# A graph layer on one core: its first two column chunks opened together, unit by unit

## The chip, the cores and the metric

The kernel runs on one core of one Trainium2 chip. The metric is the device time of one execution in microseconds (us), median of several. Beside the median stands one profiled execution, whose trace is read below. Engines are called PE (TensorE), ACT (ScalarE), DVE (VectorE), Pool (GpSimd) and SP (SyncE, which here issues the loads).

## The reference

With N = 4096 and D = 128, and one dense adjacency matrix `adj` [N, N] for both branches:

```
h   = max(layernorm(x), 0)
out1 = conv(h,  adj, eps1, W1, b1)
out2 = conv(x2, adj, eps2, W2, b2)
y   = x + concat(out1, out2) @ Wm.T + bm

conv(v, a, eps, W, b):
    ax = a @ v
    t = ax + (1 + eps) * ax
    for i in 0..2:  t = relu(t @ W[i].T + b[i])
    return t
```

Everything is float32.

## The kernel before

**Numbers.** To keep float32 accuracy, each operand of a product is split in two: a rounded part `hi` (type fp32r) and the rest `lo` = raw - hi. A product is three matmuls: lo x hi, hi x hi, hi x lo. `product` (L436 on; its matmuls are L440, L441, L444) does this.

**Tiles.** The output is made transposed, in 8 chunks of 512 columns (`CW`). For each chunk the 4096 rows to be summed are taken in 8 units of 4 blocks of 128 (`U`, `JB`). One unit of `adj` is 128 x 2048, 1 MB; it goes through a ring of 4 slots (`adj_raw`, `adj_hi`, `adj_lo`). The array `adj_tiles` holds each unit as 128 rows of 8 KB. Per unit and branch PE does 4 blocks x 3 matmuls of 512 columns, so 24 per unit and 192 per chunk, into the PSUM banks `acc[0]` and `acc[1]`. Branch 1 (x2) comes first in each unit, then branch 0 (x); after branch 0, `unit_used` frees the slot.

**Who does what for a unit.** SP loads it. ACT rounds it to `adj_hi` (L230 whole, L263 by block). DVE subtracts to `adj_lo` (L338 whole, L394 by block). PE multiplies.

**Features.** `feat_hi` and `feat_lo` hold all 32 blocks of both branches and are made once, during chunk 0, one unit of 4 blocks at a time. x2: ACT rounds (L268), Pool subtracts (L203). x: DVE takes `bn_stats`, `bn_aggr`, adds epsilon (L362, L365, L367); ACT the square root (L273); DVE a reciprocal with one Newton step (L373 to L378); ACT applies scale, shift and relu (L280, `rectify`) and rounds (L283); Pool subtracts (L207).

**Order of the work.** Each engine has its own instruction stream, written by hand, and the streams meet at semaphores. Chunk 0 is unrolled. In it SP issues, for each unit, x, x2 and then the unit of adj; the first three units (`FINE_LOADS`) are loaded as four DMAs of 256 KB, each 2 KB out of every 8 KB row. ACT does for each unit: x2's rounding, the square root, four adj_hi of 512 columns, `rectify`. DVE does: `variances`, `scale_and_shift`, four adj_lo of 512. PE's `first_aggregate` (L464, L470, L480) takes first all hi x hi of a unit and branch, then feat_lo x hi, then hi x adj_lo. Before the first product PE does 12 matmuls on zeros (`WARM_UP`, L550).

**Layers.** When a chunk's sums are ready, ACT drains them from PSUM twice, as `act_hi` and `act_f` (L246, L247, `branch_operand`), DVE makes `act_lo` (L344), and PE does a layer of both branches (6 matmuls, `layer`) after units 1, 3 and 5 of the next chunk and the merge after unit 6. `acc` is one pair of banks, so the first product of a chunk waits for `act_f` of the chunk before. The last chunk has an order of its own, with the second branch's layers in quarters of 128 columns. The weights are split by Pool after chunk 0's features (L210, L212).

Of the kernel before, what the change touches and what calls it, by code (L numbers as in the profile page):

```python
# [6 lines left out]
def gnn_layer_kernel(nc, adj_tiles, x_tiles, x2_tiles, x_t, w_t, bias_t, eps, out_t):  # L7
# [4 lines left out]
    ALU = mybir.AluOpType  # L12
# [5 lines left out]
    CW = 512  # L18
# [24 lines left out]
    OPERAND_AFTER = {1: 0, 3: 1, 5: 2, 7: 3}  # L43

# [11 lines left out]
    with ExitStack() as ctx:  # L56
# [46 lines left out]
        hidden_quarter = [hidden[0], bank("hidden_quarter1"), hidden[1], bank("hidden_quarter3")]  # L103
# [55 lines left out]
        def _(sp):  # L159
            def load_unit(c, u):  # L160

                if not (isinstance(c, int) and c * U + u < RING):
                    sp.wait_ge(lo_made, c * U + (u + 1 - RING))
                sp.dma_start(adj_raw[:, u % RING, :], adj_tiles[c * U + u]).then_inc(raw_loaded[u % RING], 16)
# [7 lines left out]
            for u in range(U):  # L172
                load_x(u)
# [3 lines left out]
                if u < FINE_LOADS:  # L177
                    for j in range(JB):
                        cols = slice(j * CW, (j + 1) * CW)
                        done = fine_loaded[u * FINE_SIGNALS + j] if j < FINE_SIGNALS else raw_loaded[u]  # L180
                        sp.dma_start(adj_raw[:, u, cols], adj_tiles[u][:, cols]).then_inc(done, 16)
                else:
                    load_unit(0, u)
                if u == U - 2:
# [3 lines left out]
            with sp.Fori(1, CHUNKS) as c:  # L188
# [8 lines left out]
        def _(pool):  # L197

            for u in range(U):
# [9 lines left out]
            pool.wait_ge(w_loaded, 16)  # L209
            nc.gpsimd.tensor_copy(w_hi[:, :, :], w_raw[:, :, :]).then_inc(w_hi_made, 1)  # L210
            pool.wait_ge(w_hi_made, 1)
            nc.gpsimd.tensor_tensor(w_lo[:, :, :], w_raw[:, :, :], f32(w_hi[:, :, :]),  # L212
                                    ALU.subtract).then_inc(w_lo_made, 1)
# [11 lines left out]
        def _(act):  # L225
            def high_of_unit(c, u):
                act.wait_ge(raw_loaded[u % RING], 16 * (c * (U // RING) + (u // RING + 1)))
                if not (isinstance(c, int) and c * U + u < RING):
                    act.wait_ge(unit_used, c * U + (u + 1 - RING))
                nc.scalar.activation(adj_hi[:, u % RING, :], adj_raw[:, u % RING, :], ACT.Copy).then_inc(hi_made, 1)  # L230

            def source(m, k, b):
# [21 lines left out]
            def fine_high(u, j):  # L254
                slot, cols = u % RING, slice(j * CW, (j + 1) * CW)
                last = j == FINE_SIGNALS
                if u < FINE_LOADS and not last:
                    act.wait_ge(fine_loaded[u * FINE_SIGNALS + j], 16)
                else:
                    act.wait_ge(raw_loaded[slot], 16 * (u // RING + 1))  # L260
                if u >= RING:
                    act.wait_ge(unit_used, u + 1 - RING)
                nc.scalar.activation(adj_hi[:, slot, cols], adj_raw[:, slot, cols], ACT.Copy).then_inc(  # L263
                    hi_made if last else fine_hi_made, 1)

# [24 lines left out]
            for u in range(U):  # L290
                high_of_x2(u)
                std_of_x(u)
                for j in range(JB):
                    fine_high(u, j)
                rectify(u)
            act.wait_ge(bias_loaded, 16)
            act.wait_ge(scale_made, 1)
            with act.Fori(1, LAST) as c:
# [25 lines left out]
        def _(dve):  # L324
# [294 lines left out]
```

## Time and profile before

| | |
|---|---|
| median of 3 runs | 414.39 us (414.32 to 414.98) |
| profiled execution | 414.23 us |
| its span, first to last instruction | 412.3 us |
| PE busy | 403.9 us, 98% |
| DVE busy | 221.1 us, 54% |
| ACT busy | 219.8 us, 53% |
| chain that ended last | PE 85%, DVE 6%, ACT 5%, issue 2%, DMA 1% |
| DMA | 76.15 MB, mean 185 GB/s |

The span is what the trace covers; the execution's time is 1.93 us longer. Matmuls are pipelined, and a record shows a matmul from its start to its modelled end, so the records overlap: the pace is the distance from start to start. Where a row of the timeline merges several instructions ("x4"), its time is from the first start to the last end.

### The profile page before, as it was taken

The page shows a single profiled execution, that of the slowest core. Times are in us where ns is not written, and L with a number is a line of the kernel's source. Part 1 is how long each engine was busy: PE and PEld are TensorE (multiplying, and loading weights), DVE is VectorE, ACT ScalarE, POOL GpSimd, SP SyncE. Part 2 cuts the span into 40 slices and gives each one's busy share as a digit, 9 for nine tenths or more (in the row PEclk, how much of TensorE's full clock was granted, in tenths as well). Part 3 has the DMA queues.
Part 4 walks back from the last instruction along what each step waited for, and adds up shares of the span by engine and source line. Part 5 has one row for each costly group of instructions (what it writes and reads, how often), then busy time and mean ns, then how long its engine had stood idle before and what let it go on. Part 6 is the DMA issues. An engine that isn't in the chain of part 4 may idle for free.

```text
span 412.3 us, 5004 instructions
## 1 busy us (share of the span) xinstructions
PE 403.9 (98%) x1763; PEld 326.9 (79%) x1763; DVE 221.1 (54%) x277; ACT 219.8 (53%) x276; POOL 34.1 (8%) x37
## 2 busy tenths in 40 slices
PE   7999989999999999999999999999999999999997
PEld 2777768888888888888888888888888888888886
DVE  5899975552834447334555426455174453755223
ACT  5889892355543355543445554345553345775034
POOL 1443470000100000000100001000010000000100
PEclk9999999999999999999999999999999999999999
DMA  7998568432655517455183454833366531740100
GB/s 237 398 413 328 203 211 325 167 131 110 254 203 203 186 43 265 167 203 203 59 327 109 166 203 138 315 141 117 153 231 227 203 149 55 263 196 1 52 0 25
DMA packets 14745, 76.15 MB, mean 185 GB/s; under 512 B 2000, under 2 KB 2256, under 8 KB 6928
## 3 DMA queue, kind: packets, MB, share of 16 engines
q1 hardware_dynamic: 13392, 71.97, 46.9%
q0 software_dynamic: 1200, 3.93, 2.7%
q10 hardware_dynamic: 144, 0.13, 0.1%
q8 instruction: 5, 0.08, 0.1%
q14 instruction: 4, 0.03, 0.0%
HBM read 73.93 MB, written 2.10 MB: 184 GB/s over the span
## 4 chain that ended last, share of the span: by engine, by line
PE 85%; DVE 6%; ACT 5%; issue 2%; DMA 1%; SPq 0%; ACTq 0%; DVEq 0%
PE acc L440 25%; PE acc L444 25%; PE acc L441 25%; DVE adj_lo L394 3%; ACT adj_hi L263 3%; PE hidden L441 3%; PE hidden L440 3%; PE hidden L444 2%; DMA adj_raw<-adj_tiles 1%; DVE stats L362 1%; PE merged L441 1%; PE merged L440 1%; PE merged L444 1%; ACT x_rows L280 1%; DVE var_eps L367 1%
## 5 line engine op out<-in xcount | busy, mean ns | idle before, releaser
L440 PE MATMUL acc<-adj_hi,feat_lo 128*128 128x512 f32 x448 | 175.0, 391 | 1.6 <-ACT act_f L247 1.6
L444 PE MATMUL acc<-adj_lo,feat_hi 128*128 128x512 f32 x448 | 174.8, 390 | 0.0
L441 PE MATMUL acc<-adj_hi,feat_hi 128*128 128x512 f32 x448 | 174.2, 389 | 0.0
L338 DVE TENSOR_TENSOR adj_lo<-adj_raw,adj_hi 128x2048 fp32r<-128x2048 f32 x56 | 128.2, 2327 | 26.7 <-ACT adj_hi L230 26.7
L344 DVE TENSOR_TENSOR act_lo<-act_f,act_hi 128x512 fp32r<-128x512 f32 x60 | 41.3, 690 | 124.7 <-ACT act_f L247 124.7
L230 ACT ACTIVATE adj_hi<-adj_raw 128x2048 fp32r<-128x2048 f32 x56 | 104.8, 1928 | 2.2 <-PE acc L444 2.0
L246 ACT ACTIVATE act_hi<-hidden,bias 128x512 fp32r<-128x512 f32 x45 | 31.0, 688 | 129.1 <-PE hidden L444 129.1
L440 PEld LDWEIGHTS acc<-adj_hi,feat_lo 128*128 128x128 f32 x448 | 84.1, 188 | 19.8 <-issue 2.1
L444 PEld LDWEIGHTS acc<-adj_lo,feat_hi 128*128 128x128 f32 x448 | 84.1, 188 | 18.1
L441 PEld LDWEIGHTS acc<-adj_hi,feat_hi 128*128 128x128 f32 x448 | 84.1, 188 | 18.0
L246 ACT ACTIVATE act_hi<-acc,ax_scale 128x512 fp32r<-128x512 f32 x15 | 10.3, 687 | 44.7 <-PE acc L444 44.7
L247 ACT ACTIVATE act_f<-hidden,bias 128x512 f32<-128x512 f32 x45 | 31.0, 688 | 0.0
L219 POOL DMA_DIRECT2D out_t<-y_sb x7 | 3.8, 546 | 304.2 <-DVE y_sb L356 304.2
L394 DVE TENSOR_TENSOR adj_lo<-adj_raw,adj_hi 128x512 fp32r<-128x512 f32 x32 | 20.1, 688 | 0.7 <-ACT adj_hi L263 0.7
L464 PE MATMUL acc<-adj_hi,feat_hi 128*128 128x512 f32 x64 | 18.3, 400 | 1.4 <-ACT adj_hi L263 1.3
L356 DVE SCALAR_TENSOR_TENSOR y_sb<-merged,bias,x_res 128x512 f32<-128x512 f32 x7 | 5.3, 750 | 26.6 <-PE merged L444 26.6
L470 PE MATMUL acc<-adj_hi,feat_lo 128*128 128x512 f32 x64 | 18.0, 403 | 1.1 <-POOL feat_lo L207 1.0
L263 ACT ACTIVATE adj_hi<-adj_raw 128x512 fp32r<-128x512 f32 x32 | 17.8, 617 | 1.9 <-DMA adj_raw<-adj_tiles 1.8
L441 PE MATMUL hidden<-act_hi,w_hi 128*128 128x512 f32 x45 | 17.7, 393 | 0.0
L440 PE MATMUL hidden<-act_hi,w_lo 128*128 128x512 f32 x45 | 17.6, 391 | 0.0
L444 PE MATMUL hidden<-act_lo,w_hi 128*128 128x512 f32 x45 | 17.6, 390 | 0.0
L480 PE MATMUL acc<-adj_lo,feat_hi 128*128 128x512 f32 x64 | 17.3, 391 | 0.0
(60 smaller groups left out, 204.6 us busy)
## 6 DMA issues: line engine op xcount, KB each, us to landing
adj_raw<-adj_tiles SPq DMA_DIRECT2D x61, 1024.0 KB, 5.0
x_rows<-x_tiles SPq DMA_DIRECT2D x16, 256.0 KB, 6.4
adj_raw<-adj_tiles SPq DMA_DIRECT2D x12, 256.0 KB, 6.3
x_res<-x_t POOLq DMA_DIRECT2D x8, 256.0 KB, 6.2
out_t<-y_sb POOLq DMA_DIRECT2D x7, 256.0 KB, 2.3
w_raw<-w_t SPq DMA_DIRECT2D x1, 512.0 KB, 9.1
out_t<-y_sb SPq DMA_DIRECT2D x1, 128.0 KB, 1.8
out_t<-y_sb ACTq DMA_DIRECT2D x1, 128.0 KB, 1.8
```

The costliest lines, as they stand in the source:

```text
L230: nc.scalar.activation(adj_hi[:, u % RING, :], adj_raw[:, u % RING, :], ACT.Copy).then_inc(hi_made, 1)
L246: nc.scalar.activation(act_hi[:, b, :], src[:, :], **how).then_inc(act_hi_made[b], 1)
L247: nc.scalar.activation(act_f[:, b, :], src[:, :], **how).then_inc(act_f_made[b], 1)
L263: nc.scalar.activation(adj_hi[:, slot, cols], adj_raw[:, slot, cols], ACT.Copy).then_inc(hi_made if last else fine_hi_made, 1)
L338: nc.vector.tensor_tensor(adj_lo[:, u % RING, :], adj_raw[:, u % RING, :], f32(adj_hi[:, u % RING, :]), ALU.subtract).then_inc(lo_made, 1)
L344: nc.vector.tensor_tensor(act_lo[:, b, :], act_f[:, b, :], f32(act_hi[:, b, :]), ALU.subtract).then_inc(act_lo_made[b], 1)
L394: nc.vector.tensor_tensor(adj_lo[:, slot, cols], adj_raw[:, slot, cols], f32(adj_hi[:, slot, cols]), ALU.subtract).then_inc(lo_made if las ...
L440: nc.tensor.matmul(out, lhs_lo, rhs_hi, start=start, stop=False)
L441: nc.tensor.matmul(out, lhs_hi, rhs_hi, start=False, stop=False)
L444: return nc.tensor.matmul(out, lhs_hi, rhs_lo, start=False, stop=stop)
L464: nc.tensor.matmul(acc[b][:, :], feat_hi[:, b, u * JB + j, :], adj_hi[:, s, cols], start=(u == 0 and j == 0), stop=False)
L470: nc.tensor.matmul(acc[b][:, :], feat_lo[:, b, u * JB + j, :], adj_hi[:, s, cols], start=False, stop=False)
```

## The change

The first two chunks are done together. A list `OPENING` gives the order of the 16 adj units: for feature units 0 to 5 chunk 0's adj unit and then chunk 1's; then units 6 and 7 of chunk 0, then 6 and 7 of chunk 1. PE takes them in pairs: both adj units for branch 1, then both for branch 0. Chunk 1 has banks of its own, `second_acc` (they are also the quarter banks of the end). Only the first two adj units are loaded and split by block, and these eight blocks come from a new array `adj_first`, in which each 128 x 512 block is 256 KB in one piece. Of the eight, four are of unit 0 of chunk 0 and four of unit 0 of chunk 1. The other opening units go as whole 128 x 2048 units on ACT and DVE.

SP issues x2 before x. The warm-up has 15 matmuls on zeros, and two more such matmuls (`FILLERS`) follow each of the first four products. PE's order in the first two adj units is hi x hi, hi x adj_lo, feat_lo x hi. The weights are split by ACT and DVE instead of Pool. Chunk 0's drain starts when its 14 units are used; its layers 0 and 1 lie in the last pair of the opening. Chunk 2 (`TURN`) is unrolled and carries chunk 0's layer 2 and merge, and all layers and the merge of chunk 1. From chunk 3 on the loop is as before.

```diff
-def gnn_layer_kernel(nc, adj_tiles, x_tiles, ...
+def gnn_layer_kernel(nc, adj_tiles, adj_first, x_tiles, ...
-    FINE_LOADS = 3
+    FINE_LOADS = 2
-    WARM_UP = 12
+    WARM_UP = 15
+    FILLERS = 2
+    OPENING = [(u, c) for u in range(U - 2) for c in range(2)]
+    OPENING += [(u, c) for c in range(2) for u in (U - 2, U - 1)]
+    USED_AFTER = [OPENING.index((U - 1, c)) + 1 for c in range(2)]
+    TURN = 2
+    TURN_LAYER_AFTER = {0: (0, 2), 2: (1, 0), 3: (1, 1), 4: (1, 2)}
+    TURN_MERGE_AFTER = {1: 0, 5: 1}
+    TURN_OPERAND_AFTER = {3: (0, 2), 4: (0, 3), 5: (1, 0), 6: (1, 1), 7: (1, 2)}
...
+        second_acc = [bank(f"second_acc{b}") for b in range(2)]
+        hidden_quarter = [hidden[0], second_acc[0], hidden[1], second_acc[1]]
...
             # SP
+            for s, (u, c) in enumerate(OPENING):
+                if c == 0:
+                    load_x2(u)
+                    load_x(u)
+                if s < FINE_LOADS:
+                    for j in range(JB):
...
+                        sp.dma_start(adj_raw[:, s, cols], adj_first[s * JB + j]).then_inc(done, 16)
+                else:
+                    if s >= RING:
+                        sp.wait_ge(lo_made, s + 1 - RING)
+                    sp.dma_start(adj_raw[:, s % RING, :], adj_tiles[c * U + u]).then_inc(raw_loaded[s % RING], 16)
...
             # Pool
-            nc.gpsimd.tensor_copy(w_hi[:, :, :], w_raw[:, :, :]).then_inc(w_hi_made, 1)
...
             # ACT
+            for u in range(U - 2):
+                high_of_x2(u)
+                std_of_x(u)
+                high_of_opening(2 * u)
+                high_of_opening(2 * u + 1)
+                rectify(u)
...
+            nc.scalar.activation(w_hi[:, :, :], w_raw[:, :, :], ACT.Copy).then_inc(w_hi_made, 1)
...
+            branch_operand(0, 0, first)
+            high_of_unit(TURN, 0)
+            branch_operand(0, 0, late)
+            high_of_unit(TURN, 1)
+            operand(0, 1)
+            for u in range(2, U):
+                high_of_unit(TURN, u)
+                if u in TURN_OPERAND_AFTER:
+                    operand(*TURN_OPERAND_AFTER[u])
+            operand(1, STEPS - 1)
...
             # DVE
+            for u in range(U - 2):
+                variances(u)
+                scale_and_shift(u)
+                low_of_opening(2 * u)
+                low_of_opening(2 * u + 1)
...
             # PE
+            idle_products(WARM_UP)
+            for s in range(0, len(OPENING), 2):
+                for b in BRANCH_ORDER:
+                    for at in (s, s + 1):
+                        if at < FINE_LOADS:
+                            fine_aggregate(at, b)
+                        else:
+                            opening_aggregate(at, b)
+                    if s == len(OPENING) - 2:
+                        layer(0, 0 if b == first else 1)
             for u in range(U):
                 for b in BRANCH_ORDER:
-                    first_aggregate(u, b)
-            with pe.Fori(1, LAST) as c:
+                    aggregate(TURN, u, b)
+                if u in TURN_LAYER_AFTER:
+                    layer(*TURN_LAYER_AFTER[u])
+                if u in TURN_MERGE_AFTER:
+                    merge(TURN_MERGE_AFTER[u])
+            with pe.Fori(TURN + 1, LAST) as c:
```

`fine_aggregate` is the old block-by-block form in its new order, with `idle_products(FILLERS)` behind each hi x hi of adj unit 0, first branch; `opening_aggregate` is the `aggregate` of the later chunks, with waits on `feat_hi` and `feat_lo` of its unit.

## Rows read from the trace of the kernel before

**Rows 1.** The page: its head and PE's busy time.

```profile
span 412.3 us, 5004 instructions
...
PE 403.9 (98%) x1763; PEld 326.9 (79%) x1763; DVE 221.1 (54%) x277; ACT 219.8 (53%) x276; POOL 34.1 (8%) x37
```

**Rows 2.** Waits of PE: us in total, times, longest us.

```profile
PE acc L470 <- POOL feat_lo L207: 1.0, 6, 0.2
```

**Rows 3.** Windows: length, busy us (count) of PE, PEld, DVE, ACT, POOL; clock, DMA, GB/s.

```profile
4.00:7.00 3.00, 2.75 (x8) 0.77 (x6) 2.52 (x13) 1.42 (x3) 1.26 (x1) 1.00 0.89 227
...
15.00:20.00 5.00, 5.00 (x24) 4.11 (x22) 4.59 (x16) 3.99 (x10) 2.55 (x2) 1.00 1.04 404
...
100.00:350.00 250.00, 250.00 (x1099) 205.97 (x1098) 122.46 (x87) 121.71 (x121) 5.83 (x11) 1.00 0.48 178
```

**Rows 4.** Timeline of PE at the start: start, us, what, [idle before <-releaser].

```profile
1.44 5.30 PE L550 MATMUL merged<-zeros 128*128 128x512 bf16 x12 [1.44 <-DVE zeros L397]
...
6.99 0.58 PE L464 MATMUL acc<-adj_hi,feat_hi 128*128 128x512 f32 x1 [0.25 <-ACT adj_hi L263]
...
9.07 1.12 PE L464 MATMUL acc<-adj_hi,feat_hi 128*128 128x512 f32 x2 [0.15 <-ACT adj_hi L263]
10.03 1.09 PE L470 MATMUL acc<-adj_hi,feat_lo 128*128 128x512 f32 x4
...
11.89 1.19 PE L464 MATMUL acc<-adj_hi,feat_hi 128*128 128x512 f32 x4
```

**Rows 5.** Timeline of PE: units 2 and 7 of chunk 0, and the turn.

```profile
24.64 1.19 PE L470 MATMUL acc<-adj_hi,feat_lo 128*128 128x512 f32 x4
...
54.26 1.20 PE L470 MATMUL acc<-adj_hi,feat_lo 128*128 128x512 f32 x4 [0.16 <-POOL feat_lo L207]
55.29 1.07 PE L480 MATMUL acc<-adj_lo,feat_hi 128*128 128x512 f32 x4
58.00 0.49 PE L440 MATMUL acc<-adj_hi,feat_lo 128*128 128x512 f32 x1 [1.63 <-ACT act_f L247]
```

**Rows 6.** Timeline of DVE over one unit, and a subtraction of Pool.

```profile
22.79 0.87 DVE L362 BATCH_NORM_STATS2 stats<-x_rows 128x6 f32<-128x128 f32 x4
...
26.36 2.50 DVE L394 TENSOR_TENSOR adj_lo<-adj_raw,adj_hi 128x512 fp32r<-128x512 f32 x4
28.77 0.86 DVE L362 BATCH_NORM_STATS2 stats<-x_rows 128x6 f32<-128x128 f32 x4
...
23.30 1.29 POOL L207 TENSOR_TENSOR feat_lo<-x_rows,feat_hi 128x512 fp32r<-128x512 f32 x1 [3.45 <-ACT feat_hi L283]
```

**Rows 7.** Timeline of DVE and ACT at the start.

```profile
3.53 0.87 DVE L362 BATCH_NORM_STATS2 stats<-x_rows 128x6 f32<-128x128 f32 x4 [2.15 <-DMA x_rows<-x_tiles]
...
4.85 0.17 DVE L367 TENSOR_SCALAR var_eps<-mean_var 128x4 f32<-128x4 f32 x1
...
4.47 0.63 ACT L268 ACTIVATE feat_hi<-x_rows 128x512 fp32r<-128x512 f32 x1 [1.99 <-DMA x_rows<-x_tiles]
...
6.21 0.63 ACT L263 ACTIVATE adj_hi<-adj_raw 128x512 fp32r<-128x512 f32 x1 [0.95 <-DMA adj_raw<-adj_tiles]
7.74 1.90 ACT L263 ACTIVATE adj_hi<-adj_raw 128x512 fp32r<-128x512 f32 x3 [0.90 <-DMA adj_raw<-adj_tiles]
```

**Rows 8.** Timeline of ACT, Pool and DVE at the turn from chunk 0.

```profile
53.00 3.72 ACT L230 ACTIVATE adj_hi<-adj_raw 128x2048 fp32r<-128x2048 f32 x2 [0.17 <-issue]
56.63 0.66 ACT L246 ACTIVATE act_hi<-acc,ax_scale 128x512 fp32r<-128x512 f32 x1
...
55.27 4.31 POOL L212 TENSOR_TENSOR w_lo<-w_raw,w_hi 128x1024 fp32r<-128x1024 f32 x1
...
55.05 6.68 DVE L338 TENSOR_TENSOR adj_lo<-adj_raw,adj_hi 128x2048 fp32r<-128x2048 f32 x2 [2.40 <-ACT adj_hi L230]
```

**Rows 9.** The page's groups: busy us, mean ns of one, idle before and its releaser.

```profile
L338 DVE TENSOR_TENSOR adj_lo<-adj_raw,adj_hi 128x2048 fp32r<-128x2048 f32 x56 | 128.2, 2327 | 26.7 <-ACT adj_hi L230 26.7
L344 DVE TENSOR_TENSOR act_lo<-act_f,act_hi 128x512 fp32r<-128x512 f32 x60 | 41.3, 690 | 124.7 <-ACT act_f L247 124.7
L230 ACT ACTIVATE adj_hi<-adj_raw 128x2048 fp32r<-128x2048 f32 x56 | 104.8, 1928 | 2.2 <-PE acc L444 2.0
```

More of the change, by code:

```diff
@@ L169, in load_x, with load_x2 @@
                 sp.dma_start(x_rows[:, u % X_SLOTS], x_tiles[u]).then_inc(x_loaded[u % X_SLOTS], 16)
-            for u in range(U):
-                load_x(u)
+            def load_x2(u):
                 if u >= X_SLOTS:
@@ new lines, in low_of_opening @@
+            def low_of_opening(s):
+                if s < FINE_LOADS:
+                    for j in range(JB):
+                        fine_low(s, j)
+                    return
+                dve.wait_ge(raw_loaded[s % RING], 16 * (s // RING + 1))
+                dve.wait_ge(hi_made, s + 1)
+                if s >= RING:
+                    dve.wait_ge(unit_used, s + 1 - RING)
+                nc.vector.tensor_tensor(adj_lo[:, s % RING, :], adj_raw[:, s % RING, :], f32(adj_hi[:, s % RING, :]),
+                                        ALU.subtract).then_inc(lo_made, 1)
@@ L404, in _ @@
+            for u in (U - 2, U - 1):
+                low_of_opening(OPENING.index((u, 1)))
+            dve.wait_ge(w_hi_made, 1)
+            nc.vector.tensor_tensor(w_lo[:, :, :], w_raw[:, :, :], f32(w_hi[:, :, :]),
+                                    ALU.subtract).then_inc(w_lo_made, 1)
             dve.wait_ge(eps_loaded, 16)
@@ L467, in first_aggregate @@
                 pe.wait_ge(feat2_lo_made if b else feat1_lo_made, u + 1)
                 for j in range(JB):
-                    s, cols = columns(u, j)
-                    nc.tensor.matmul(acc[b][:, :], feat_lo[:, b, u * JB + j, :], adj_hi[:, s, cols],
-                                     start=False, stop=False)
-                if not fine:
-                    pe.wait_ge(lo_made, u + 1)
-                for j in range(JB):
-                    if fine and j < FINE_SIGNALS:
-                        pe.wait_ge(fine_lo_made, u * FINE_SIGNALS + j + 1)
-                    elif fine:
-                        pe.wait_ge(lo_made, u + 1)
-                    s, cols = columns(u, j)
-                    last = nc.tensor.matmul(acc[b][:, :], feat_hi[:, b, u * JB + j, :], adj_lo[:, s, cols],
-                                            start=False, stop=(u == U - 1 and j == JB - 1))
+                    slot, cols = columns(s, j)
@@ new lines, in fine_aggregate, with opening_aggregate @@
+                    last = nc.tensor.matmul(out[:, :], feat_lo[:, b, u * JB + j, :], adj_hi[:, slot, cols],
+                                            start=False, stop=False)
+                signal(u, b, last)
+            def opening_aggregate(s, b):
+                u, c = OPENING[s]
+                out = opening_bank(c, b)
+                pe.wait_ge(hi_made, s + 1)
+                pe.wait_ge(feat2_hi_made if b else feat1_hi_made, u + 1)
+                pe.wait_ge(feat2_lo_made if b else feat1_lo_made, u + 1)
+                for j in range(JB):
+                    slot, cols = columns(s, j)
+                    last = product(out[:, :], feat_hi[:, b, u * JB + j, :], feat_lo[:, b, u * JB + j, :],
+                                   adj_hi[:, slot, cols], adj_lo[:, slot, cols],
+                                   start=False, stop=(u == U - 1 and j == JB - 1),
+                                   lo_ready=(lo_made, s + 1) if j == 0 else None)
```

145 lines of the change are left out of this document (80 added, 65 removed).

## The prediction

> **What bounds the kernel now.** I read the page's head first. TensorE (PE) is busy for 403.9 of the 412.3 us [rows 1], so an edit can only gain where PE starts late, stands still or runs below its usual pace. A busy PE is not PE at its peak, so the next view is the windows, for the pace: in the long middle 1099 matmuls take 250 us [rows 3], 0.2275 us each. All of them have 512 columns, and the granted clock there is the upper level, 2.4 GHz. At this pace a unit (24 matmuls, both branches) takes 5.46 us and a chunk (192) 43.68 us.
>
> The PE timeline then shows the only stretch that is worse. Chunk 0's first product starts at 6.99 [rows 4] and chunk 1's at 58.00 [rows 5]: 51.01 us for 43.68 us of work, so 7.3 us are lost after the first product. They lie in three places.
> - The first branch of unit 0 runs from 6.99 to 11.89 for 12 matmuls worth 2.73: 2.2 lost. The products follow the adj blocks as ScalarE (ACT) rounds them [rows 4, 7].
> - From unit 2 on a unit takes (54.26 - 24.64) / 5 = 5.92 instead of 5.46 [rows 5], and the same 0.46 or so is lost in unit 1 and in each of the six after it: some 3.2 in all. The chain of waits names PE's releaser (Pool's feat_lo [rows 2]), but that is only the last link. VectorE (DVE) is what has this period: from one stats group to the next 28.77 - 22.79 = 5.98 [rows 6], full of work. It does 2.4 us of adj_lo (26.36 to 28.77) and 3.5 us of statistics and Newton steps, all once per unit.
> - At the turn the last chunk-0 product issues at 55.29 + 3 x 0.23, so PE could go on at 56.2, and goes on at 58.00: 1.8 lost. PE waits 1.63 of it for ACT's act_f [rows 5], which was behind two whole adj_hi [rows 8].
>
> **The change, part by part.** Removed and added work first. PE's products are the same in number, 8 fillers and 3 warm-up matmuls apart. The adj bytes are the same.
>
> *Two chunks per feature unit.* PE now has 48 matmuls, 10.92 us, per feature unit. DVE has 3.5 + 2 x 2.3 (the mean of a whole adj_lo [rows 9]) = 8.1 us. ACT was busy for 3.99 of 5.00 us [rows 3], so 4.7 per unit, and one more adj_hi of 1.93 [rows 9] makes 6.6. DMA brings 2.6 MB per pair, 6.5 us at 404 GB/s [rows 3]. All are below 10.92, so the 3.2 us of the unit rhythm go to zero.
>
> *The turn.* Chunk 0 closes two units before chunk 1 does, and chunk 2 starts in acc, which ACT can drain while PE works on chunk 1's last two units (10.92 us). The drain is four activations of 0.66 [rows 8], 2.6 us at most. So the 1.8 us go to zero.  In chunk 2 each layer or merge of the two chunks now comes after nearly every unit. The worst step is: ACT's adj_hi 1.93, DVE's adj_lo 2.33, two act_lo of 0.69 [rows 9], 5.6 us from the release of a slot, against the step's six matmuls plus one unit on PE, 1.4 + 5.5 = 6.8. It hides with 1.2 us to spare; without this cover it costs what it is late, at each of six steps.
>
> *w_hi and w_lo* leave Pool for ACT (about 1 us, twice the cadence of a 512-column adj_hi) and DVE (about 1.2). They are queued before branch_operand(0,0), which has about 5 us until chunk 0's second branch ends. Cost nothing. On Pool w_lo took 4.31 and held one DVE adj_lo up: two of them took 6.68 [rows 8] where two by the mean take 4.7. That ends too, but PE was not waiting for it beyond the turn.
>
> *The very start.* SP's x2 load now precedes x. Before, x was used at 3.53 and x2 at 4.47 [rows 7], so x moves to about 4.45. The variance lands 1.49 after that (5.02 - 3.53), and std and adj_hi follow: ACT's first adj_hi starts at 4.45 + 1.49 + 0.03 + 0.2 = 6.2, against 6.21 now. So the swap costs nothing, for the block lands then anyway; PE's first product is 0.78 behind it, as now [rows 4, 7]: 7.0.
> Warm-up: twelve matmuls stand 0.427 apart (5.30 less the last one's 0.6, over 11), which is the pace of 1.2 GHz. The f32 products of as many columns stand 0.23 apart at 10 us (eight from 10.03 to 11.89), the pace of 2.4 GHz. Three more end at 7.85 if all run at the lower level, at 7.2 if the clock rises where it seems to rise now, before 6.99. I take 7.2.
> The Trainium skill ("TensorE: Matmul & The Clock Gate", The HAM clock gate) says that the phase at which the clock rises varies from run to run. By that page alone the first product would lie anywhere between 7.2 and 7.9; this trace holds one phase, so it cannot confirm it.
>
> *Unit 0 after the first product*, from both sides. The unknown is the landing of the contiguous 256 KB blocks; no adj block of this shape is in the trace. Slow end, as now: ACT starts blocks at 6.21 and 7.74 and then every 0.52 to 0.63 [rows 7]; PE reaches the fourth at 9.69 (10.19 less 0.5), restarts (0.34, to 10.03), runs two fillers (0.43) and is at 10.4; DVE, started at 7.2, has the fourth adj_lo by 10.3; eight matmuls to 12.2. The second chunk's blocks have landed by 11.6 (four more after the x pair, 0.65 each at 404 GB/s), so 12 more matmuls end at 15.0. Fast end, by the nearest contiguous rows (x to x2, 0.94 apart [rows 7]): blocks at 5.4, 6.3, 7.0, 7.7; ACT no longer waits; PE is held by the fillers at one product per 0.66 from 7.2, and by DVE (four adj_lo from 7.2, done 9.7); then 9.8, 11.6, 14.3. In 4 to 7 us DMA moves only 227 GB/s, against 404 later [rows 3], and I can't tell how much of this is the stride. Each restart after a wait costs another 0.11 (0.34 against 0.23), which the fast end leaves out, some four times.
> The fillers lie in time in which PE would wait. With that cover gone they would cost 8 x 0.22 = 1.8.
>
> *Later pairs.* The second branch of pair 0 needs feat1: ACT free by 10.9 to 12.2, rectify 2.3, ready at 13.2 to 14.5, before 14.3 to 15.0. Pair 1 starts on PE at 19.8 to 20.5. Its 1 MB blocks land by 15.5 and 18.1 (2.6 each); adj_hi by 17.4 and 20.0; adj_lo by 19.7 and 22.4; wanted from 20.3 and 23.0. Spare: 0.6 us and more, and growing by 2 us and more per pair after that.
>
> **The sum.** First 24 matmuls done at 14.3 to 15.0; 168 more at 0.2275 are 38.2: 52.5 to 53.2 stands where 58.00 stood. The gain is 4.8 to 5.5; I take 5.0, nearer the slow end for the restarts. The profiled execution took 414.23, span 412.3 and 1.93 around it; so 409.2. The median of the runs is 414.39, 0.16 above that execution, so the forecast is 409.4.
>
> **Rivals.** 0.2% is 0.83 us, about what a measurement of this kernel tells from no change.
> 1. *As forecast*, 408.8 to 410.0: chance 0.60.
> 2. *The first pairs run dry.* DVE now does both fine units before unit 1's variances, and ACT's adj_hi of pair 1 is queued behind the std that needs them. Spare there is only 0.6 us, and the 256 KB blocks moved slowly at first. If the first megabytes come at 227 GB/s for 3 us longer, pair 1 is late by some 1.3, and up to 2: 410.3 to 411.5. For: the thin margin. Against: 404 GB/s from 15 us on. Chance 0.15.
> 3. *A late clock.* Warm-up at 0.427 to the end: first product at 7.85, and the first four products are paced by ACT anyway: 0.65 more, 1.5 with a few slow products: 410.1 to 410.9. The fillers speak against it. Chance 0.08.
> 4. *The start is better still*: ACT is never kept waiting and restarts vanish, 5.6 to 6.3 gained: 408.1 to 408.8. For: the low DMA rate at 4 to 7. Against: fillers and DVE hold that end. Chance 0.09.
> 5. *DVE bounds the pairs*, so that the gain goes back: each of the six later pairs would have to take 10.92 + 5.0 / 6 = 11.75 on DVE for no gain, and 11.9 for slower by 0.2%. From rows: 8.1 plus both feat_lo of Pool (1.29 each [rows 6]) if each stops DVE in full, 10.7. This is under 10.92. The Trainium skill ("SBUF — State Buffer", SBUF: two separate sides) calls the port pair of the two engines an exclusive lock for a whole instruction; the 6.68 us beside Pool's 4.31 agree, and by that rule 10.7 is the most. Chance 0.04: 413.6 to 416, half of it above 415.2.
> 6. *Chunk 2's steps are late* by 1 us each, giving back the gain, slower from 0.98 each on: a step must take 7.8, not 5.6. Chance 0.04, for 413.6 to 416, again half of it above 415.2.
>
> Faster (cases 1 to 4) 0.92, same 0.04, slower 0.04. The range 408.4 to 411.0 holds cases 1, 3, most of 4 and half of 2: 0.8.
>
> **What would show it.** PE timeline: first product 7.0 to 7.4, 24 products by 14.3 to 15.0, then 0.2275 apart with no wait over 0.2 us until chunk 2 starts, 53.2 + 43.7 + 2.7 for two layers, near 99.5; no wait for act_f. DVE has idle time in each pair. If PE waits for adj_lo or adj_hi between 19 and 31 us, rival 2 holds; if matmuls after 7.85 are 0.427 apart, rival 3; if waits recur every 10.9 us, rival 5. The prediction would be wrong if the rest of the run, from chunk 2 on, were not the same to 0.3 us.

## The result and the profile after

The changed kernel takes 408.26 us (median, 408.12 to 408.85) against 414.41 for the kernel before: ratio 0.9849, interval 0.9836 to 0.9861. In a later series it took 408.50 against 414.56, ratio 0.9854 (0.9835 to 0.9873). The forecast was 409.4, in a range of 408.4 to 411.0. So the direction came as written, and both losses that the change was to remove are gone; but the gain of 6.1 us was larger than the 5.0 forecast, the median lies 0.14 us below the range, and the reason that was given for one of the two losses was wrong. All eight executions of the two series together have a median of 408.36, also just below the range.

The profiled execution took 408.38, with a span of 406.9. PE's list of waits (us in total, times, longest us) has one line left, where before it had four; ACT's adj_hi, Pool's feat_lo [rows 2] and the turn's act_f [rows 5] are gone from it:

```profile
PE merged L514 <- DVE zeros L441: 1.4, 1, 1.4
```

The chain that ended last, by engine:

```profile
PE 99%; DVE 0%; issue 0%; DVEq 0%
```

The PE timeline, to be read against [rows 4]:

```profile
1.44 5.64 PE L514 MATMUL merged<-zeros 128*128 128x512 bf16 x15 [1.44 <-DVE zeros L441]
6.79 0.51 PE L534 MATMUL acc<-adj_hi,feat_hi 128*128 128x512 f32 x1
7.15 0.60 PE L514 MATMUL merged<-zeros 128*128 128x512 bf16 x2
7.64 0.49 PE L534 MATMUL acc<-adj_hi,feat_hi 128*128 128x512 f32 x1
...
9.59 1.28 PE L544 MATMUL acc<-adj_lo,feat_hi 128*128 128x512 f32 x4
10.71 1.09 PE L549 MATMUL acc<-adj_hi,feat_lo 128*128 128x512 f32 x4
11.63 1.07 PE L534 MATMUL second_acc<-adj_hi,feat_hi 128*128 128x512 f32 x4
...
14.35 1.07 PE L534 MATMUL acc<-adj_hi,feat_hi 128*128 128x512 f32 x4
...
19.79 0.39 PE L506 MATMUL acc<-adj_hi,feat_lo 128*128 128x512 f32 x1
...
98.75 0.39 PE L506 MATMUL acc<-adj_hi,feat_lo 128*128 128x512 f32 x1
```

The first product starts at 6.79 (6.99 before), the 25th at 14.35, the 49th at 19.79, chunk 2 at 98.75. From 14.35 on nothing waits. The windows (columns as in [rows 3]) give the pace of the opening:

```profile
4.00:7.00 3.00, 3.00 (x11) 1.21 (x9) 2.12 (x14) 1.17 (x4) 1.26 (x1) 1.00 0.98 307
...
14.35:96.00 81.65, 81.65 (x361) 67.60 (x361) 61.60 (x111) 56.40 (x75) 20.99 (x16) 1.00 0.77 290
100.00:350.00 250.00, 250.00 (x1099) 205.94 (x1098) 122.00 (x91) 125.34 (x131) 6.50 (x12) 1.00 0.48 176
```

81.65 us for 361 matmuls is 0.2262; the middle of the run is as before, 1099 in 250 us. The 193rd product starts at 52.43 (14.35 + 168 x 0.2267), where chunk 1's first stood at 58.00: 5.6 us of the gain are there. They divide at two marks: 0.2 before the first product (6.99 to 6.79); 0.66 in the first 24 (8.22 us before, 15.21 being the start of the 25th; 7.56 now); 4.7 in the next 168 (42.8 before, 38.1 now). From there to the issue of the last store, the first of these lines before and the second now, the two kernels take the same to 0.14 us (351.65 and 351.51):

```profile
409.65 0.35 SPq L192 DMA_DIRECT2D out_t<-y_sb  x1
...
403.94 0.35 SPq L211 DMA_DIRECT2D out_t<-y_sb  x1
```

ACT and DVE at the start, against [rows 7]; a second block that is there at 6.96 instead of 7.74 is the thing to see:

```profile
5.93 0.20 ACT L293 ACTIVATE std<-var_eps 128x4 f32<-128x4 f32 x1 [1.52 <-DVE var_eps L405]
6.04 0.61 ACT L273 ACTIVATE adj_hi<-adj_raw 128x512 fp32r<-128x512 f32 x1
6.96 1.88 ACT L273 ACTIVATE adj_hi<-adj_raw 128x512 fp32r<-128x512 f32 x3 [0.31 <-DMA adj_raw<-adj_first]
```

### The profile page after: what moved, and what is told of

It is laid out like the page before. It is cut to its first block, busy times and chain, and to the rows that moved or that the text cites. A ratio compares the mean times of both kernels' runs of the same rounds, so it can differ in the third digit from the quotient of the medians.

```text
span 406.9 us, 4872 instructions
## 1 busy us (share of the span) xinstructions
PE 402.3 (99%) x1774; PEld 328.7 (81%) x1774; DVE 219.5 (54%) x260; ACT 220.2 (54%) x259; POOL 30.2 (7%) x35
## 4 chain that ended last, share of the span: by engine, by line
PE 99%; DVE 0%; issue 0%; DVEq 0%
PE acc L510 25%; PE acc L506 25%; PE acc L507 25%; PE second_acc L506 3%; PE second_acc L510 3%; PE second_acc L507 3%; PE hidden L507 3%; PE hidden L506 3%; PE hidden L510 3%; PE merged L514 2%; PE merged L507 1%; PE merged L506 1%; PE merged L510 1%; PE acc L534 0%; PE acc L549 0%; PE acc L544 0%
## 5 line engine op out<-in xcount | busy, mean ns | idle before, releaser
L506 PE MATMUL acc<-adj_hi,feat_lo 128*128 128x512 f32 x440 | 171.8, 390 | 0.0
L510 PE MATMUL acc<-adj_lo,feat_hi 128*128 128x512 f32 x440 | 171.7, 390 | 0.0
L507 PE MATMUL acc<-adj_hi,feat_hi 128*128 128x512 f32 x440 | 171.1, 389 | 0.0
L376 DVE TENSOR_TENSOR adj_lo<-adj_raw,adj_hi 128x2048 fp32r<-128x2048 f32 x48 | 108.3, 2288 | 37.9 <-ACT adj_hi L243 36.9
L243 ACT ACTIVATE adj_hi<-adj_raw 128x2048 fp32r<-128x2048 f32 x48 | 90.4, 1926 | 17.6 <-PE acc L510 15.8
L507 PEld LDWEIGHTS acc<-adj_hi,feat_hi 128*128 128x128 f32 x440 | 82.6, 188 | 17.7
L510 PEld LDWEIGHTS acc<-adj_lo,feat_hi 128*128 128x128 f32 x440 | 82.6, 188 | 17.8
L438 DVE TENSOR_TENSOR adj_lo<-adj_raw,adj_hi 128x2048 fp32r<-128x2048 f32 x14 | 31.7, 2290 | 7.8 <-ACT adj_hi L284 7.8
L284 ACT ACTIVATE adj_hi<-adj_raw 128x2048 fp32r<-128x2048 f32 x14 | 26.3, 1905 | 1.7 <-DMA adj_raw<-adj_tiles 0.9
L506 PE MATMUL second_acc<-adj_hi,feat_lo 128*128 128x512 f32 x56 | 21.8, 389 | 0.0
L510 PE MATMUL second_acc<-adj_lo,feat_hi 128*128 128x512 f32 x56 | 21.8, 389 | 0.0
L507 PE MATMUL second_acc<-adj_hi,feat_hi 128*128 128x512 f32 x56 | 21.8, 389 | 0.0
```

Source lines behind the costliest of these rows:

```text
L284: nc.scalar.activation(adj_hi[:, s % RING, :], adj_raw[:, s % RING, :], ACT.Copy).then_inc(hi_made, 1)
L376: nc.vector.tensor_tensor(adj_lo[:, u % RING, :], adj_raw[:, u % RING, :], f32(adj_hi[:, u % RING, :]), ALU.subtract).then_inc(lo_made, 1)
L438: nc.vector.tensor_tensor(adj_lo[:, s % RING, :], adj_raw[:, s % RING, :], f32(adj_hi[:, s % RING, :]), ALU.subtract).then_inc(lo_made, 1)
L506: nc.tensor.matmul(out, lhs_lo, rhs_hi, start=start, stop=False)
L507: nc.tensor.matmul(out, lhs_hi, rhs_hi, start=False, stop=False)
L510: return nc.tensor.matmul(out, lhs_hi, rhs_lo, start=False, stop=stop)
```

## The experiments

Times are medians. The kernel before took 414.73, 414.43, 414.64 and 414.56 in the four series, runs 1 to 4, 5 to 8, 9 to 12 and 13 to 16.

### 1. The changed kernel with blocks from the old array

```diff
-   sp.dma_start(adj_raw[:, s, cols], adj_first[s * JB + j]).then_inc(done, 16)
+   sp.dma_start(adj_raw[:, s, cols], adj_tiles[c * U + u][:, cols]).then_inc(done, 16)
```

> The changed kernel, but its first eight blocks come from the old array again, 2 KB out of every 8 KB. Theory (the one-piece blocks land earlier, and the first 24 products are paced by their landing): the second block lands near 7.7 again instead of 6.9, the 25th product starts near 15.0 instead of 14.35, and the time is 0.5 to 0.8 us above the changed kernel's, 408.8 to 409.1. Rival (the layout does nothing; the order of the loads and the warm-up made the fast end): within 0.2 us of the changed kernel, 408.3.

Measured: 409.61 (409.37 to 409.92), 1.35 above the changed kernel, more than the theory said. Timeline of PE and ACT, and the window:

```profile
8.44 0.49 PE L534 MATMUL acc<-adj_hi,feat_hi 128*128 128x512 f32 x1 [0.58 <-ACT adj_hi L273]
...
15.75 1.20 PE L534 MATMUL acc<-adj_hi,feat_hi 128*128 128x512 f32 x4
...
7.76 0.63 ACT L273 ACTIVATE adj_hi<-adj_raw 128x512 fp32r<-128x512 f32 x1 [0.96 <-DMA adj_raw<-adj_tiles]
...
4.00:7.00 3.00, 2.79 (x11) 1.03 (x9) 2.19 (x15) 1.03 (x3) 1.26 (x1) 1.00 0.76 208
```

From 4 to 7 us DMA moves 208 GB/s with strided blocks and 307 with one-piece blocks; the second block is used at 7.76 and not at 6.96, and the 25th product comes at 15.75 and not at 14.35. The theory holds in kind, the rival is out, and my slow end (15.0) was too fast for a strided load. One profile per kernel is thin for a rate, so here are all of them, 4 to 7 us: 201 to 277 GB/s in the nine profiles with strided blocks (mean 229), 252 to 346 in the nine with one-piece blocks (mean 316), the low 252 being run 2.

### 2, 12. Without the fillers, and with the old warm-up as well

```diff
-    FILLERS = 2
+    FILLERS = 0          # run 2: WARM_UP stays 15; run 12: WARM_UP = 12
```

> The changed kernel without the two idle matmuls behind each of the first four products. Theory (they lie in time in which PE would wait, and VectorE's fourth adj_lo at about 9.6 holds the next products anyway): the same time to 0.2 us, 408.3, and PE shows waits for adj_hi again. Rival A (they cost PE time: 8 x 0.22): 0.4 to 1.7 us faster. Rival B (they keep the clock at 2.4 GHz): products after 7 us at 0.427 spacing and 0.5 us or more slower.

> The changed kernel with 12 warm-up matmuls and no idle ones between the products. Theory (the fillers did nothing, but three warm-up matmuls fewer leave PE idle before the first product, and the clock falls in some executions; in the changed kernel PE has no slack to swallow it): mean clock below 0.998 in some executions and 1 to 2.5 us more in those, median 408.2 to 410.5. Rival (the clock holds without them too): 408.3 in all executions.

Measured: run 2 408.21 (407.82 to 408.37), mean clock 0.999 or 1.0 in all five executions. In its profile PE waits 0.2 us for adj_hi, as said. The fillers cost nothing and gain nothing beside 15 warm-up matmuls, as far as five executions show. Run 12 has a median of 407.98, but a spread: four executions with a mean clock of 0.999 or 1.0 took 407.65 to 408.17, one with 0.996 took 409.57, one with 0.992 took 410.79. So the clock can fall in the changed kernel too, and here the fall is paid for: 1.6 and 2.8 us above that median. That the three warm-up matmuls are what prevents it is likely but not shown: two falls in six executions stand against none in the five of run 2.

### 3, 4. x before x2; the weights split by Pool

```diff
 # run 3, SP
-    load_x2(u)
     load_x(u)
+    load_x2(u)
...
 # run 4, Pool, behind its feat_lo
+    nc.gpsimd.tensor_copy(w_hi[:, :, :], w_raw[:, :, :]).then_inc(w_hi_made, 1)
...
 # run 4, ACT (and the same for w_lo on DVE)
-    nc.scalar.activation(w_hi[:, :, :], w_raw[:, :, :], ACT.Copy).then_inc(w_hi_made, 1)
```

> The changed kernel with x loaded before x2, as the kernel before had it. Theory (the second block's landing and the warm-up hold the start, not the variances): x lands near 3.6, ScalarE starts adj_hi at 5.3 instead of 6.04, but the 25th product still starts within 0.3 us of 14.35; time 408.0 to 408.5. Rival (the x path sets the first product): 0.5 us or more faster, 407.7.

> The changed kernel with the weights split by GpSimd, as before. Theory (moving them was worth nothing to PE, as chunk 0's first layer comes late): the same time to 0.2 us, 408.3; VectorE shows one adj_lo of about 4.4 us instead of 2.3 beside GpSimd's w_lo. Rival (w_lo is late for the first layer, or the held-up adj_lo reaches PE): PE waits at the first layer, 0.5 to 2 us slower.

Measured: 408.68 (408.08 to 409.27) and 408.44 (408.20 to 409.02), both medians within the spread of the changed kernel, the first 0.2 above its forecast. The 25th product starts at 14.07 and 14.19. In run 4 two adj_lo take 7.01 us beside Pool's w_lo, and PE waits for neither. No worth of either part by itself can be seen here.

### 5, 8. One-piece blocks in the kernel before

```diff
-   sp.dma_start(adj_raw[:, u, cols], adj_tiles[u][:, cols]).then_inc(done, 16)
+   sp.dma_start(adj_raw[:, u, cols], adj_first[u * JB + j]).then_inc(done, 16)
```

> The kernel before with one part of the change alone: its first twelve adj blocks come from an array in which each lies in one piece. Theory (the blocks land earlier, which unit 0 gains): chunk 1's first product starts 0.5 to 0.9 us earlier than 58.00; time 413.5 to 413.9. Rival (layout does nothing): 414.4.

> The kernel before with the one-piece blocks once more, one look for a second profile of the landing times. Theory: the first adj block lands by 5.4 and the second by 7.0, in this profile as in the other. Rival: the landing varies by 0.5 us or more from one profile to the next.

Run 8 is the same kernel as run 5, for a second profile; its label says otherwise. Measured: 413.39 (ratio 0.9974, 0.9965 to 0.9983) and 413.38: 1.0 us faster. Chunk 1's first product starts at 57.36 and 57.10, so 0.6 and 0.9 earlier than 58.00, as the theory had it. ACT uses the first block at 5.35 and 5.11, the second at 6.47 and 6.03: within run 8's theory, though the two profiles are 0.4 apart. In run 5 the mean clock is 0.999 or 1.0 in ten of eleven executions, which it rarely is in the kernel before; by run 9 below that is not where the time comes from. The window from 4 to 7 us in run 5:

```profile
4.00:7.00 3.00, 2.21 (x8) 0.76 (x6) 2.48 (x12) 1.89 (x4) 1.27 (x1) 1.00 0.96 322
```

### 6, 11. The turn by itself

Run 6 drains chunk 0 ahead of chunk 1's adj_hi. Run 11 makes the first adj_hi, drains, makes the second, and takes the weights off Pool.

```diff
 # run 6, ACT, chunk 1 written out
+    branch_operand(0, 0, first)
+    high_of_unit(1, 0)
+    branch_operand(0, 0, late)
+    high_of_unit(1, 1)
...
 # run 11, ACT; DVE makes w_lo behind low_of_unit(1, 1), and Pool nothing of the weights
+    high_of_unit(1, 0)
+    branch_operand(0, 0, first)
+    branch_operand(0, 0, late)
+    high_of_unit(1, 1)
+    nc.scalar.activation(w_hi[:, :, :], w_raw[:, :, :], ACT.Copy).then_inc(w_hi_made, 1)
```

> The kernel before, but at the turn ScalarE drains chunk 0's first branch before it makes chunk 1's adj_hi, and the second branch before the second adj_hi. Theory (the turn lost 1.8 us, because act_f stood behind two whole adj_hi): PE's wait of 1.63 us is gone or below 0.3, time 412.6 to 413.0. Rival (the wait comes back at the next step, since adj_hi or adj_lo of chunk 1 is now late): 414.0 or more.

> The kernel before with the turn mended in another order: ScalarE makes chunk 1's first adj_hi, drains both branches of chunk 0, then makes the second adj_hi, and w_hi and w_lo are made behind it by ScalarE and VectorE instead of GpSimd. Theory (the first attempt failed since adj_hi came late and GpSimd's w_lo held VectorE's adj_lo up): PE's wait at the turn is 0.6 us or less, time 412.9 to 413.4. Rival (adj_lo is the wall at this turn in any order): a wait of 1.3 us or more, 414.0 or more.

Run 6 took 417.08 (ratio 1.0059, 1.0045 to 1.0072), 2.6 us slower. The rival had it. Timeline at the turn, then windows:

```profile
56.05 2.39 POOL L212 TENSOR_TENSOR w_lo<-w_raw,w_hi 128x1024 fp32r<-128x1024 f32 x1
...
57.28 5.51 DVE L346 TENSOR_TENSOR adj_lo<-adj_raw,adj_hi 128x2048 fp32r<-128x2048 f32 x2 [3.84 <-PE acc L488]
...
57.53 0.40 PE L449 MATMUL acc<-adj_hi,feat_hi 128*128 128x512 f32 x1
...
60.63 0.50 PE L452 MATMUL acc<-adj_lo,feat_hi 128*128 128x512 f32 x1 [2.71 <-DVE adj_lo L346]
```

```profile
10.00:13.00 3.00, 2.82 (x7) 2.09 (x7) 2.53 (x11) 2.97 (x7) 0.32 (x1) 0.52 1.06 402
...
61.50:64.50 3.00, 3.00 (x9) 2.32 (x7) 3.00 (x4) 2.35 (x2) 0.00 (x0) 0.50 0.96 319
```

PE has act_f at 57.20, and then stands 2.71 us for adj_lo: adj_hi came late, because it was behind the drain, and DVE's adj_lo then met Pool's w_lo. PE goes on at 60.63 at its old pace, but from 61.5 to 64.5 the granted clock reads 0.50, the 1.2 GHz level, and the matmuls start 0.427 apart instead of 0.2275: a second price, about 1.6 us, for one idle stretch.

Run 11 took 413.99 (0.9982, 0.9973 to 0.9991), 0.65 faster. PE at its turn:

```profile
56.65 0.39 PE L454 MATMUL acc<-adj_hi,feat_lo 128*128 128x512 f32 x1
56.88 0.39 PE L455 MATMUL acc<-adj_hi,feat_hi 128*128 128x512 f32 x1
...
57.55 0.50 PE L458 MATMUL acc<-adj_lo,feat_hi 128*128 128x512 f32 x1 [0.29 <-DVE adj_lo L343]
```

0.45 us of the turn's 1.8 are left (56.88 to 57.55, less 0.23). The time missed its forecast by 0.6: of the 1.35 won at the turn only 0.65 is in the median. The profile shows where the rest went in its own execution. In this profile the last unit's feat_lo products came at 54.70 and not at 54.26 [rows 5]: the fourth block of adj was used only at 9.45, Pool's feat_lo of unit 0 started at 12.36 where it was 11.92 before, and the one of unit 7 at 53.36 where it was 52.91. The 0.44 from the first loads stood unchanged through the whole chunk. And the last two stores took 2.5 and 2.6 us to land where both took 1.8 before, 0.8 at the very end. Whether the other executions had the same two losses is not shown.

### 7, 9, 10, 13. Who has the rhythm of chunk 0

```diff
 # runs 7, 10, 13: no Newton step
-    step(nc.vector.reciprocal(r0, std[:, :]))
-    step(nc.vector.tensor_tensor(nt, r0, r0, ALU.mult))
-    step(nc.vector.scalar_tensor_tensor(nt, nt, -0.5, var_eps[:, :], ALU.mult, ALU.mult))
-    step(nc.vector.scalar_tensor_tensor(rstd[:, :], nt, 1.5, r0, ALU.add, ALU.mult))
+    step(nc.vector.reciprocal(rstd[:, :], std[:, :]))
 # runs 9, 10, 13: the clock's guard
-    WARM_UP = 12
+    WARM_UP = 15
+    FILLERS = 2
 # run 13: no var_eps on DVE
-    nc.vector.tensor_scalar(var_eps[:, :], mean_var[:, :, 1], LN_EPS, None, ALU.add).then_inc(var_made, 1)
-    nc.scalar.activation(std[:, :], var_eps[:, :], ACT.Sqrt).then_inc(std_made, 1)
+    nc.scalar.activation(std[:, :], mean_var[:, :, 1], ACT.Sqrt, bias=ln_eps[:, 0:1]).then_inc(std_made, 1)
...                                                # ln_eps is filled once; bn_aggr now signals var_made
```

> The kernel before without the Newton step on rstd: the reciprocal is used as it is, so the layernorm is a little less exact. Three small VectorE operations per unit go, about 1.2 us of its 5.9. Theory (VectorE has the 5.92 us period of chunk 0's units, and GpSimd's feat_lo is only the last link): the period falls to PE's 5.46 and chunk 1 starts 2.5 to 3.3 us earlier, time 411.2 to 411.9. Rival (GpSimd, or the rounding of x on ScalarE, has the period, as the list of waits names it): the period stays above 5.8, 414.0 or more.

Run 7: 413.70 (0.9982), only 0.7 faster; by the time my theory fell. But the windows showed two things at once: PE at full pace from 16 to 55 us, and a clock at its lower level ahead of it:

```profile
9.00:15.80 6.80, 6.50 (x15) 4.66 (x15) 5.77 (x16) 6.42 (x16) 3.04 (x2) 0.50 1.04 388
16.00:55.00 39.00, 38.93 (x172) 31.87 (x171) 34.02 (x95) 33.34 (x71) 17.32 (x14) 1.00 0.82 315
```

The first does not mean that the period is gone. Pool's feat_lo still starts every 5.93 us, and PE, late by the slow stretch, has caught up with it at the end of the chunk:

```profile
47.03 1.29 POOL L207 TENSOR_TENSOR feat_lo<-x_rows,feat_hi 128x512 fp32r<-128x512 f32 x1 [3.38 <-ACT feat_hi L283]
52.96 1.30 POOL L207 TENSOR_TENSOR feat_lo<-x_rows,feat_hi 128x512 fp32r<-128x512 f32 x1 [3.38 <-ACT feat_hi L283]
54.31 1.19 PE L466 MATMUL acc<-adj_hi,feat_lo 128*128 128x512 f32 x4
```

The next two runs kept the clock up.

> The kernel before with the change's 15 warm-up matmuls and two idle matmuls behind each of the first four products, nothing else. The two runs before this one lost TensorE's 2.4 GHz for 3 to 7 us after about 9 us. Theory (VectorE has the rhythm of chunk 0, so a fall of the clock there is swallowed): the mean clock rises to 0.999 or 1.0 in every execution, and the time stays within 0.4 us of 414.4. Rival (the fall is paid in full in the kernel before, and guarding it is a good part of the gain): 1.0 us or more faster, 413.4.

> The kernel before with the guard of the clock (15 warm-up matmuls, two idle ones behind each of the first four products) and without the Newton step, so the layernorm is a little less exact. Theory (with VectorE relieved no unit waits, and what hid this in the run without the guard was the clock): clock 0.999 or 1.0, no recurring wait from unit 1 to unit 7, 411.2 to 411.9. Rival (relieving VectorE is worth 0.7 us as measured, and the clock was no part of it): 413.3 to 413.8.

Run 9: 414.90 (ratio 1.0001, 0.9992 to 1.0010), mean clock 1.0 in all 11 executions. In the same series all 27 executions of the kernel before had 0.991 to 0.996, at 414.64; the profile that the rows of before come from, with a clock of 1.00, is of the rarer kind. The kernel before thus loses the upper clock in most executions (68 of the 72 in the four series are below 0.998) and pays nothing that can be measured. What swallows it is PE's room of 0.46 us in each unit: in run 7 PE made good a stretch of 6.8 us at the lower level, as its rows above show. Run 10: 413.91, clock 0.999 or 1.0, and waits at 36.18, 42.09, 48.02 and 53.94, still 5.92 apart, with 1.2 us of DVE's work gone. The theory of run 10 is refuted; DVE's load does not set the period. Of the 0.7 us that runs 7 and 10 did gain, 0.3 is at the turn, where PE waits 1.34 and 1.36 us for act_f instead of 1.63; the rest was not followed up. One unit of its timeline shows what does:

```profile
34.84 1.29 POOL L208 TENSOR_TENSOR feat_lo<-x_rows,feat_hi 128x512 fp32r<-128x512 f32 x1 [3.39 <-ACT feat_hi L284]
...
35.12 1.03 DVE L368 TENSOR_SCALAR var_eps<-mean_var 128x4 f32<-128x4 f32 x1
...
36.19 0.20 ACT L274 ACTIVATE std<-var_eps 128x4 f32<-128x4 f32 x1 [0.90 <-DVE var_eps L368]
36.30 2.18 ACT L264 ACTIVATE adj_hi<-adj_raw 128x512 fp32r<-128x512 f32 x4
...
38.38 1.63 ACT L281 ACTIVATE x_rows<-x_rows,shift,rstd 128x128 f32<-128x128 f32 x4
...
40.05 0.63 ACT L284 ACTIVATE feat_hi<-x_rows 128x512 fp32r<-128x512 f32 x1
...
40.76 1.28 POOL L208 TENSOR_TENSOR feat_lo<-x_rows,feat_hi 128x512 fp32r<-128x512 f32 x1 [3.38 <-ACT feat_hi L284]
```

It is a ring. Pool's feat_lo starts (34.84); DVE's var_eps of the next unit, 4 elements wide, starts beside it and ends with it, 1.03 us where alone it takes 0.17; ACT's square root waits for it; behind that stand ACT's four adj_hi, rectify and rounding; and that rounding starts the next feat_lo, at 40.76: 5.92. The Trainium skill ("SBUF — State Buffer", SBUF: two separate sides) calls the port pair of the two engines an exclusive lock held for a whole instruction. The 1.03 for 0.17 agrees. DVE looked full in the rows of before because time in which an operation is held counts as busy. There the hold of var_eps is shorter, as the Newton step makes DVE arrive later, but it ends with Pool's feat_lo (29.21 + 1.29) all the same:

```profile
30.09 0.44 DVE L367 TENSOR_SCALAR var_eps<-mean_var 128x4 f32<-128x4 f32 x1
```

So in the kernel before, DVE had 0.27 us in hand in each period (0.44 less 0.17), and its own cycle would be some 5.65 us by that, an estimate: a close second to the ring. The last run takes the one locked operation out of the ring.

> The kernel before with the guard of the clock, without the Newton step and without VectorE's var_eps operation: ScalarE adds the epsilon inside its square root, so nothing of VectorE between statistics and square root waits beside GpSimd's feat_lo. The layernorm is a little less exact. Theory (a ring: GpSimd's feat_lo 1.28, in which var_eps is held up, then ScalarE's square root, four adj_hi, rectify and rounding, 4.55, then feat_lo again; 5.92 in all, whatever else VectorE does): ScalarE's idle time of 0.90 before the square root falls to below 0.3, the period to PE's 5.46, no recurring wait; 410.8 to 411.9. Rival (the period is another engine's or the loads'): still 5.8 or more, 413.5 or more.

Measured: 410.61 (410.38 to 411.05), ratio 0.9905 (0.9889 to 0.9921), 3.9 faster than before and 3.3 faster than run 10. Its timeline:

```profile
34.15 1.29 POOL L209 TENSOR_TENSOR feat_lo<-x_rows,feat_hi 128x512 fp32r<-128x512 f32 x1 [3.19 <-ACT feat_hi L285]
...
39.28 1.29 POOL L209 TENSOR_TENSOR feat_lo<-x_rows,feat_hi 128x512 fp32r<-128x512 f32 x1 [2.59 <-ACT feat_hi L285]
...
44.95 1.29 POOL L209 TENSOR_TENSOR feat_lo<-x_rows,feat_hi 128x512 fp32r<-128x512 f32 x1 [3.12 <-ACT feat_hi L285]
...
40.28 0.30 ACT L275 ACTIVATE std<-mean_var,ln_eps 128x4 f32<-128x4 f32 x1 [0.55 <-DVE mean_var L367]
```

Two lengths of the ring now take turns, 5.13 and 5.67 here; from 23.34 to 50.15 the mean is 5.36, below PE's 5.46. ACT's wait before the square root is 0.55 to 0.62 in every second unit (I had said under 0.3) and none in the others. PE has no recurring wait. The ring is shown for the kernel without its Newton step. No run takes var_eps alone out of the kernel before; by the 5.65 above its units would then still be a little longer than PE's 5.46.

### 14, 15, 16. The time around the span

```diff
 # run 14, the changed kernel
+        spare = [sem(f"spare{k}") for k in range(12)]
...
 # run 15, the kernel before, PE
+            for u in range(U):
+                for b in BRANCH_ORDER:
+                    aggregate(1, u, b)
...
-            with pe.Fori(1, LAST) as c:
+            with pe.Fori(2, LAST) as c:
```

> The changed kernel with twelve more semaphores that nothing uses. Theory (time around the span grows with semaphores; the kernel before has three more than the changed one): the time less the span rises from 1.5 to 2 us or more. Rival (it has nothing to do with them): 1.5 as before, time 408.3.

> The kernel before with chunk 1 of TensorE's loop written out, as the changed kernel has its opening chunks. Theory (the time around the span hangs on the length of TensorE's written-out stream): the time less the span falls from 1.9 to about 1.5, time 414.0. Rival (it does not): 1.9, time 414.4 to 414.6.

> The changed kernel once more, for more executions beside these. Expected: 408.1 to 408.6, time less span 1.5, mean clock 0.999 or 1.0 in every execution. If it is 408.4 or above at the median, the miss of the range by 0.14 us is no more than the choice of runs.

Time less span, over the executions: run 14 1.45 to 1.55, run 15 1.78 to 1.96, run 16 1.47 to 1.53. Both theories fell; medians 408.49, 414.51 and 408.50. Run 16 had said that a median of 408.4 or more would make the miss of the range no more than the choice of runs. It came to 408.50; the eight executions together, at 408.36, leave the miss at 0.04 us.

## Why the prediction was right and where it fell short

**The 168 products after the first 24: right in size.** It foresaw 3.2 us from the unit rhythm and 1.8 from the turn, less what of this lies in the first 24, and none left; 4.7 came, and no wait was left. From the 193rd product on the run was the same to 0.3 us, as required.

**The reason given for the rhythm: wrong.** The step "VectorE (DVE) is what has this period ... full of work" failed: runs 7 and 10 took a fifth of that work away and the period stayed at 5.92 to 5.93. It is the ring of run 10. That the forecast survived this is luck in part: two adj units per feature unit put the ring on the safe side too, and the prediction had not worked it out. DVE's period in the changed kernel, by its aggregates:

```profile
40.87 0.38 DVE L403 BATCH_NORM_AGGREGATE mean_var<-stats 128x2 f32<-128x6 f32 x4
41.28 1.20 DVE L405 TENSOR_SCALAR var_eps<-mean_var 128x4 f32<-128x4 f32 x1
...
49.92 0.38 DVE L403 BATCH_NORM_AGGREGATE mean_var<-stats 128x2 f32<-128x6 f32 x4
```

9.05 us per pair, not the 8.1 of the sum of work, with var_eps still held (1.20); PE's 10.9 covers it. The margin is 1.8 us and not 2.8.

**The turn: right here, and more delicate than I wrote.** I called it "behind two whole adj_hi" and would have mended it by order alone. Run 6 shows that the drain and adj_hi of the next unit compete for ACT in those 2 us; run 11 that 0.45 stays even in the best order tried. Opening two chunks takes both out of this place. "DVE held up, but PE was not waiting" for the weights is right in the changed kernel (run 4).

**The miss, added up.** Forecast 409.4, measured 408.26: 1.14 us. It is made of 0.45 in the first 24 products, 0.13 in the pace of the next 168 (0.2267 for 0.2275), 0.14 from there to the last store, 0.14 from the last store to the end, and 0.28 between profiled execution and median. The next three paragraphs take the terms that are not mere pace.

**The first 24 products: the term that was mis-sized most.** The sum took a place between 14.3 and 15.0, "nearer the slow end for the restarts", so 14.8. It was 14.35, the fast end, and 14.00 to 14.61 in the six other profiles with one-piece blocks in this kernel. The first product came before its 7.0 to 7.4 too, at 6.79. The one-piece blocks do what the fast end assumed: 1.35 us in the changed kernel (run 1) and 1.0 in the one before (run 5). That is 0.45 of the miss. With 14.35 alone put right the forecast would have been 408.95, inside the range, so the other terms were needed to leave it.

**1.93 us around the span: also mis-sized.** I carried it over as a constant. In the profiled execution it is 1.48 (408.38 less 406.9); it is 1.45 to 1.57 in 33 of 35 executions of the changed kernel and its variants (1.71 and 1.72 in two of run 4), and 1.56 to 2.03, mostly 1.8 to 2.0, in the kernel before and its variants. But little of these 0.45 us is a gain, for the span of the changed kernel ends later behind its last store: 2.96 us after the issue at 403.94, where it was 2.65 after the one at 409.65. The two parts together are 4.58 before and 4.44 now, so 0.14. Neither spare semaphores nor a longer written-out PE stream make the difference; what does stays open.

**Which execution.** The median of before was 0.16 above its profiled execution, that of the changed kernel 0.12 below: the remaining 0.28. It is the choice of executions. In the later series the median was 408.50, inside the range.

**The late clock.** I gave it 0.08 as a delay of the first product. It did not come. What run 12 shows is another thing, a clock that falls again after the start: up to 2.8 us in an execution. The moment of the rise does vary: the warm-up matmuls start 0.427 apart up to 3.98 in the profiles of runs 4 and 16 and up to 6.11 in the changed kernel's, and closer after that. The Trainium skill ("TensorE: Matmul & The Clock Gate", The HAM clock gate) says that the phase at which the clock rises varies between runs, and by that the first product would move. The traces agree on the rise. The first product hardly followed it: in the seven profiles with 15 warm-up matmuls it stood between 6.62 and 7.43, only run 2's inside the prediction's 7.2 to 7.9, and where the clock rose early PE waited 0.6 us for adj_hi instead (runs 4 and 16, first product at 6.84).

**Rival 4** has the measured time, 408.1 to 408.8, at a chance of 0.09. Its reason is half right: the low DMA rate at 4 to 7 us was for the most part the stride, but ACT still waited 0.31 and 0.41 us for blocks, and the 25th product came no earlier than the fast end. More than half of the miss lay elsewhere, in terms that no rival named, so that it had the time is luck in part.

**Rivals 2, 5 and 6** did not occur: nothing waited between 19 and 31 us, nor in chunk 2, which began at 98.75 for the 99.5 foreseen.

## What to carry to other kernels

A period is not explained by the engine whose busy time adds up to it; an operation that is held up counts as busy. Follow one turn of it around all engines; a small operation that is held up beside another engine's can be the link, and taking work off the busiest engine then changes nothing. When an opening is paced by making operands, giving PE twice the work per operand hides the whole ring without mending any link of it. And before an idle stretch is removed, ask what it was swallowing: a kernel without slack pays for a clock that falls.

## What the runs showed of the hardware

- Early in the run, 256 KB blocks of 2 KB rows move faster when they lie in one piece than at a stride of 8 KB: from 4 to 7 us 316 GB/s against 229 in the mean of nine profiles each, though single profiles overlap (252 to 346 and 201 to 277). From 15 to 20 us the profiles of both kernels and of runs 1 and 5 show 404 to 419, whatever the first blocks were. Why only early is not shown.
- A DVE operation of 4 elements takes 1.03 to 1.22 us when Pool's subtraction starts just ahead of it, and 0.17 alone.
- The moment at which the clock rises in the warm-up lies anywhere from 4.0 to 6.5 us in these profiles, by the distance of the matmuls (0.427, then about half); the column of the granted clock reads 1.00 all the while.
- In runs 6, 7, 11 and 15, variants of the kernel before, the granted clock fell to 1.2 GHz after the first sparse products (0.50 to 0.52 in windows from 9 or 10 us on), at no cost to the time that run 9 could find. A stall of 2.7 us in the middle (run 6) was followed within 1 us by 3 us at that level.
- The last store of 128 KB landed 1.8 us after its issue in the profiles of both kernels and 2.5 in run 11: 0.8 us of a run's time that no engine's work explains.
